# Other queues and another order for the first loads and first products of a graph layer kernel

## Chip, core and metric

One NeuronCore of a Trainium2 chip runs the kernel. The metric is the device time of one execution, in microseconds (us).

## What is computed

64 graphs of 128 nodes, 256 features each, dense weighted adjacency, fp32. Shortened from the reference:

```python
def L0(X, A):                                   # graph attention, 3 hops
    Xw = X @ Wv + bv
    sj, si = Xw @ aw[:d, 0], Xw @ aw[d:, 0]
    e = leaky_relu(sj[:, None, :] + si[:, :, None] + ab[0], 0.2)
    alpha = A * exp(e)
    transition = alpha / (sum(alpha, -1, keepdims=True) + 1e-12)
    H, Xk = 0, X
    for k in range(3):
        H = H + Xk @ Wk[k] + bk[k]
        Xk = einsum('bij,bjd->bid', transition, Xk)
    return relu(H)
x = layernorm(x + L0(x, adj))
x = layernorm(x + einsum('bnm,bmf->bnf', adj, x) @ w)
```

## The kernel before, in words

The 64 graphs are worked on in 32 pairs (`PAIRS`, `PER = 2`). The hops are computed from the inside: H is X W0 + T (X W1 + T (X W2)) with T the transition matrix, so "hop 2" is X times Wk[2], "hop 1" X times Wk[1] added to alpha times that, "hop 0" X times Wk[0] added to alpha times the sum. The projection Wv is folded with the vector aw into two columns u (`ps_u`, `score_weights()`), which stand as columns 256 and 257 of W1 and WY, so that a hop's product gives the scores too; the constant part of the scores is `shift`. The steady products run in pairs of rounded numbers: each fp32 operand is split into a high part (`_hi`, fp32r) and a rest (`_lo`), and three products stand for one (`product()`, L1050). The first pair's hops are made from the unsplit fp32 operands (`first_hop2()`, `first_hop1()`, `first_product()` L1075), which takes two instructions for each product and chunk.

There is no loop at run time. Every engine has its own list of instructions, written out by hand and held together by semaphores:

- SyncE (L304 to L394) issues nearly all loads and stores, in order; a wait ahead of a load holds all loads behind it.
- ScalarE (L397 on) issues four loads at its start (WY_sb, vectors, bk, ab), then makes the high parts (`xt_hi`, `wx_hi`, `v2_hi`, `alpha_hi_of`), the scores, Prelu (`leaky_of`) and Exp (`exponentials`).
- VectorE (L591 on) makes the low parts (`v2_lo`, `v1_lo`, WX_lo, WY_lo), scales by row sums, adds residuals, gathers statistics. Its first instructions, ahead of its helpers, copy `ps_u` and split WY and W0 (L594 to L603).
- GpSimd (L904 on) writes the identity matrix and constants, the ones columns of V2_hi, the products for the shift (L1022 to L1028), then XT_lo (L951), alphas of pairs from 1 on and small normalisation steps.
- TensorE (L1049 on) starts with nine warm-up products of constants (`keep_warm`, L1211), then the first pair as in L1295 to L1313, then `step(k)` for each pair.

The loads of pair 0 and the weights: SyncE loads xt(0), WvT, W1 (`load_Wk(1)`), waits for xt(0), loads W0, xt(1), waits for WY, loads adjs(0), waits for W1, and loads the rest. `y_done` counts hop 2 of a pair, `v1_done` hop 1, `u_done` and `u_ready` the columns u, `bias_done` the sum of the biases (a product of ones and bk). `some` is a constant of ones.

Of the kernel before, what the change touches and what calls it, by code (L numbers as in the profile page):

```python
# [5 lines left out]
F32 = mybir.dt.float32  # L6
F32R = mybir.dt.float32r
ALU = mybir.AluOpType
ACT = mybir.ActivationFunctionType

P = 128
PER = 2
DMA = 16
# [5 lines left out]
def resnorm_graph_kernel(nc, xt, adjs, nodes, WvT, vectors, ab, Wk, bk, w, si_rows, out):  # L19
    PAIRS = nodes.shape[0]  # L20
    D = w.shape[0]
# [4 lines left out]
    with ExitStack() as ctx:  # L26
# [277 lines left out]
        def _(sp):  # L304
            def load_xt(k):
                if k == 4:

                    sp.wait_ge(v1_done, 1)
                if k >= 4:
                    sp.wait_ge(xt_lo_ready, k - 3)  # L310
                sp.dma_start(xt_sb[k % 4][:], xt[k]).then_inc(xt_loaded[k % 4], DMA)
# [38 lines left out]


            load_xt(0)
            sp.dma_start(WvT_sb[:], WvT.rearrange("(c p) n -> p c n", p=P)).then_inc(WvT_loaded, DMA)
            load_Wk(1)
            sp.wait_ge(xt_loaded[0], DMA)
            load_Wk(0)
# [38 lines left out]

        @block.scalar
        def _(act):  # L397
            act.dma_start(WY_sb[:, :, 0:D], Wk[2].rearrange("(c p) n -> p c n", p=P)).then_inc(Wk_loaded[2], DMA)
            act.dma_start(vectors_sb[:].rearrange("p c n -> p (c n)"), vectors).then_inc(vectors_loaded, DMA)
            act.dma_start(bk_sb[:], bk).then_inc(bk_loaded, DMA)  # L400
            act.dma_start(ab_col[:], ab.partition_broadcast(P)).then_inc(ab_loaded, DMA)

            def xt_hi(k):

                act.wait_ge(xt_loaded[k % 4], loads(k, 4))
                act.activation(XT_hi[k % 7][:].rearrange("p c b i -> p (c b i)"),  # L406
                               xt_sb[k % 4][:], ACT.Copy).then_inc(xt_hi_ready, 1)

            def wx_hi(n):
                act.wait_ge(Wk_loaded[n], DMA)  # L410
                act.activation(WX_hi[:, :, 1 - n], (W0_sb, W1_sb)[n][:, :, 0:D], ACT.Copy).then_inc(WX_hi_ready[n], 1)
# [6 lines left out]
            def first_scores():  # L418

                act.wait_ge(v1_done, 1)  # L420
                act.wait_ge(shift_ready, 1)
                act.activation(scores[0][:].rearrange("p n b -> p b n"), ps_v[:, :, D:D + 2], ACT.Identity,
                               bias=shift[:]).then_inc(scores_ready, 1)

            def v2_hi(k):
                if k == 0:
                    act.wait_ge(y_done, 1)

                act.activation(V2_hi[k % 4][:, :, 0:D], hop2(k)[:, :, 0:D], ACT.Copy).then_inc(v2_hi_ready, 1)
# [13 lines left out]
            def exponentials(k):  # L443
                act.wait_ge(leaky_ready, k + 1)
                if k == 1:
                    act.wait_ge(first_alpha_ready, 1)
                if k > 1:
                    act.wait_ge(alpha_ready, k - 1)
                act.activation(exps[:], leaky[:], ACT.Exp).then_inc(exp_ready, 1)  # L449
# [103 lines left out]
                    late_sum_of(LAST - 3)  # L553

            xt_hi(0)
            wx_hi(0)
            v2_hi(0)
            xt_hi(1)
            first_scores()
            xt_hi(2)  # L560
            leaky_of(0)
            exponentials(0)
            xt_hi(3)
            alpha_hi_of(0)
            wx_hi(1)
            scores_of(1)
            v2_hi(1)
# [22 lines left out]
        @block.vector  # L590
        def _(dve):  # L591
            dve.memset(ones[:], 1.0).then_inc(ones_ready, 1)

            dve.wait_ge(u_done, 1)  # L594
            dve.tensor_copy(W1_sb[:, :, D:D + 2], ps_u).then_inc(u_ready, 1)
            dve.tensor_copy(WY_sb[:, :, D:D + 2], ps_u).then_inc(u_ready, 1)
            dve.wait_ge(u_ready, 2)
            dve.wait_ge(Wk_loaded[2], DMA)
            dve.tensor_copy(WY_hi[:], WY_sb[:]).then_inc(WY_hi_ready, 1)
            dve.wait_ge(WY_hi_ready, 1)  # L600
            dve.tensor_tensor(WY_lo[:], WY_sb[:], WY_hi[:].bitcast(F32), ALU.subtract).then_inc(WY_ready, 1)
            dve.wait_ge(WX_hi_ready[0], 1)
            dve.tensor_tensor(WX_lo[:, :, 1], W0_sb[:], WX_hi[:, :, 1].bitcast(F32), ALU.subtract).then_inc(WX_ready[0], 1)  # L603

            def shift_of_scores():
                dve.wait_ge(shift_done, 1)
                dve.wait_ge(ab_loaded, DMA)
# [245 lines left out]
            def split_w():  # L853
# [2 lines left out]
                dve.wait_ge(w_hi_ready, 1)  # L856
                dve.tensor_tensor(w_lo[:], w_sb[:], w_hi[:].bitcast(F32), ALU.subtract).then_inc(w_ready, 1)

            shift_of_scores()
            v2_lo(0)  # L860
            bias_of_hops()
            first_hop1()
            first_alpha()
            first_hop0()
            first_alpha_lo()
            v2_lo(1)
            inverse(0)
            first_v()
# [33 lines left out]

        @block.gpsimd
        def _(pool):  # L904
            pool.memset(identity[:], 0.0).then_inc(pool_setup, 1)
            pool.wait_ge(pool_setup, 1)
            pool.affine_select(out=identity[:], in_=identity[:], compare_op=ALU.not_equal, fill=1.0, base=0,
# [141 lines left out]
        def _(pe):  # L1049
# [242 lines left out]
                    aggregate(k - 1)  # L1292
                hop2_and_scores(k + 5, [1] if k == 1 else range(PER))

            keep_warm(ps_v[:, 0], 9)  # L1295
            first_hop2(0)
            score_weights()
            first_hop2(1)
            first_hop1(0)
            score_shift()  # L1300
            first_hop1(1)
            sum_of_biases()
            pe.wait_ge(identity_ready, 1)
            spread_scores(0)
            hop0(0)
            hop2_and_scores(1)
            pe.wait_ge(ones_columns_ready, 1)
# [59 lines left out]
```

## Time and profile before

| | us |
|---|---|
| median of 3 runs | 275.37 |
| lowest, highest | 274.53, 275.59 |
| profiled execution, its own time | 274.77 |
| its span, first to last instruction | 273.0 |

The profile shows one execution. Times in its rows are us from the start of the span unless marked ns. PE is TensorE (PEld its weight loads), DVE VectorE, ACT ScalarE, POOL GpSimd, SP SyncE; a q behind a name is the engine's queue of issued transfers. A row of a timeline has start, duration, engine, line, operation, output and inputs, count, and in brackets the idle time before it and what ended it. Matmuls are pipelined: a row lasts longer than the step to the next.

| engine | busy us | share of the span |
|---|---|---|
| TensorE | 266.3 | 98% |
| VectorE | 218.0 | 80% |
| ScalarE | 187.8 | 69% |
| GpSimd | 194.8 | 71% |

### The profile page before, as it was taken

Reading aid. Unit: us, or ns where it says so; the run is one execution under the profiler, and the core shown is the slowest. Engines: PE = TensorE matmul, PEld = TensorE weight load, DVE = VectorE, ACT = ScalarE, POOL = GpSimd, SP = SyncE. Lnnn points to the kernel's source line nnn. Section 1 sums busy time; section 2 is a strip of 40 time slices with the busy share of each in tenths; the row PEclk is TensorE's granted clock in tenths of the full one; section 3 lists DMA queues with packets and bytes.
Section 4 is the critical chain, followed back from the end, with each engine's and each line's share of the span. In section 5 each row is a group of like instructions: output and inputs, shape, how many; then the busy total and the mean of one; then the engine's idle time right before and its main releaser. Section 6 shows DMA issues by size and latency. Waiting matters only on the chain.

```text
span 273.0 us, 6038 instructions
## 1 busy us (share of the span) xinstructions
PE 266.3 (98%) x1899; PEld 247.3 (91%) x1899; DVE 218.0 (80%) x613; ACT 187.8 (69%) x427; POOL 194.8 (71%) x419
## 2 busy tenths in 40 slices
PE   7999999999999999999999999999999999999992
PEld 4899999999999999999999999999999999999991
DVE  0877698888889888888988888898888889688984
ACT  2788667777666777766677776667777666666652
POOL 2566548777877777787777878777788877557664
PEclk9999999999999999999999999999999999999999
DMA  7958347647488389454973488654994449722304
GB/s 209 275 174 95 73 115 123 141 117 149 151 144 117 100 135 148 155 154 143 135 97 104 150 154 148 137 156 89 90 168 90 117 115 115 115 66 77 118 2 154
DMA packets 28614, 34.91 MB, mean 128 GB/s; under 512 B 7075, under 2 KB 16422, under 8 KB 28582
## 3 DMA queue, kind: packets, MB, share of 16 engines
q1 hardware_dynamic: 27872, 33.99, 59.3%
q10 hardware_dynamic: 710, 0.53, 0.6%
q8 instruction: 15, 0.25, 0.4%
q14 instruction: 17, 0.14, 0.3%
HBM read 26.09 MB, written 8.42 MB: 126 GB/s over the span
## 4 chain that ended last, share of the span: by engine, by line
PE 94%; DVE 2%; DMA 2%; POOL 0%; issue 0%; ACT 0%; DVEq 0%
PE ps_v L1053 30%; PE ps_y L1053 16%; PE ps_out L1053 14%; PE ps_h L1053 11%; PE ps_agg L1224 10%; PE ps_v L1161 3%; PE ps_v L1165 3%; PE ps_v L1163 3%; DMA WY_sb<-Wk_dram 2%; PE ps_agg L1053 1%; PE ps_y L1079 1%; PE ps_v L1079 1%; DVE WX_lo L870 0%; DVE ps_v L634 0%; PE ps_y L1208 0%; POOL late_rstd L989 0%
## 5 line engine op out<-in xcount | busy, mean ns | idle before, releaser
L963 POOL TENSOR_TENSOR alpha<-exps,adjs 128x256 f32<-128x256 f32 x31 | 22.9, 738 | 35.4 <-ACT exps L449 35.4
L1053 PE MATMUL ps_v<-WX_hi,XT_hi 128*128 128x512 f32 (+1 forms) x128 | 47.7, 372 | 0.0
L1053 PE MATMUL ps_v<-WX_lo,XT_hi 128*128 128x512 f32 (+1 forms) x128 | 47.4, 371 | 0.0
L1053 PE MATMUL ps_v<-WX_hi,XT_lo 128*128 128x512 f32 (+1 forms) x128 | 47.3, 370 | 0.0
L951 POOL TENSOR_TENSOR XT_lo<-xt,XT_hi 128x512 fp32r<-128x512 f32 x32 | 41.5, 1297 | 3.0 <-ACT XT_hi L406 1.6
L481 ACT ACTIVATE y<-res,offset,rstd 128x256 f32<-128x256 f32 x62 | 33.6, 591 | 0.9 <-POOL offset L922 0.9
L967 POOL TENSOR_TENSOR alpha_lo<-alpha,alpha_hi 128x256 fp32r<-128x256 f32 x31 | 22.8, 736 | 15.9 <-ACT alpha_hi L458 15.9
L1053 PE MATMUL ps_y<-WY_hi,XT_hi 128*128 128x258 f32 x112 | 34.1, 304 | 0.0
L1224 PEld LDWEIGHTS ps_agg<-adjs,y 128*128 128x128 f32 x248 | 32.0, 191 | 2.2
L1224 PE MATMUL ps_agg<-adjs,y 128*128 128x128 f32 x248 | 32.6, 274 | 0.0
L1053 PE MATMUL ps_out<-w_hi,agg_hi 128*128 128x256 f32 x112 | 31.6, 282 | 0.0
L1053 PE MATMUL ps_y<-WY_hi,XT_lo 128*128 128x258 f32 x112 | 31.6, 282 | 0.0
L1053 PE MATMUL ps_y<-WY_lo,XT_hi 128*128 128x258 f32 x112 | 31.5, 282 | 0.0
L1053 PE MATMUL ps_out<-w_hi,agg_lo 128*128 128x256 f32 x112 | 31.3, 280 | 0.0
L1053 PE MATMUL ps_out<-w_lo,agg_hi 128*128 128x256 f32 x112 | 31.3, 279 | 0.0
L466 ACT ACTIVATE ps_v<-ps_v,inv_rowsum 128x256 f32<-128x256 f32 x62 | 25.1, 444 | 8.7 <-DVE inv_rowsum L659 6.3
L474 ACT ACTIVATE V_hi<-ps_v 128x512 fp32r<-128x512 f32 x32 | 19.0, 595 | 16.4 <-PE ps_v L1053 16.2
L945 POOL TENSOR_SCALAR out_sb<-res,rstd,offset 128x256 f32<-128x256 f32 x54 | 30.0, 564 | 0.1
L1053 PEld LDWEIGHTS ps_v<-WX_hi,XT_lo 128*128 128x128 f32 x128 | 24.1, 188 | 4.6
L654 DVE TENSOR_SCALAR rowsum<-ps_v 128x2 f32<-128x2 f32 x32 | 5.0, 158 | 28.0 <-PE ps_v L1165 27.9
L1053 PEld LDWEIGHTS ps_v<-WX_hi,XT_hi 128*128 128x128 f32 x128 | 24.1, 188 | 3.6
L1053 PEld LDWEIGHTS ps_v<-WX_lo,XT_hi 128*128 128x128 f32 x128 | 24.1, 188 | 3.4
(168 smaller groups left out, 843.9 us busy)
## 6 DMA issues: line engine op xcount, KB each, us to landing
xt<-xt_dram SPq DMA_DIRECT2D x32, 256.0 KB, 5.9
nodes<-nodes_dram SPq DMA_DIRECT2D x32, 256.0 KB, 6.1
out_dram<-out_sb SPq DMA_DIRECT2D x30, 256.0 KB, 5.9
adjs<-adjs_dram SPq DMA_DIRECT2D x32, 128.0 KB, 6.0
spread<-si_rows_dram SPq DMA_DIRECT2D x29, 128.0 KB, 5.3
W_sb<-Wk_dram SPq DMA_DIRECT2D x2, 256.0 KB, 3.9
si_rows_dram<-scores SPq DMA_DIRECT2D x29, 1.0 KB, 4.1
WY_sb<-Wk_dram ACTq DMA_DIRECT2D x1, 256.0 KB, 4.1
```

Source lines behind the costliest of these rows:

```text
L466: act.activation(ps_v[:, b, 0:D], ps_v[:, b, 0:D], ACT.Copy, scale=inv_rowsum[k % 2][:, b:b + 1]).then_inc(v_scaled, 1)
L474: act.activation(V1_hi[:], ps_v[:, :, 0:D], ACT.Copy).then_inc(v1_hi_ready, 1)
L481: last = act.activation(y[k % 3][:, b], res1[:, b], ACT.Identity, bias=offset1[:, b:b + 1], scale=rstd1[:, b:b + 1])
L945: last = pool.tensor_scalar(out_sb[k % 3][:, b], res2[k % 2][:, b], rstd2[k % 3][:, b:b + 1], offset2[k % 3][:, b:b + 1], ALU.mult, ALU.add)
L951: pool.tensor_tensor(XT_lo[k % 7][:].rearrange("p c b i -> p (c b i)"), xt_sb[k % 4][:], XT_hi[k % 7][:].rearrange("p c b i -> p (c b i)") ...
L963: pool.tensor_tensor(alpha[:], exps[:], adjs_sb[k % 5][:], ALU.mult).then_inc(alpha_ready, 1)
L967: pool.tensor_tensor(alpha_lo[k % 2][:], alpha[:], alpha_hi[k % 2][:].bitcast(F32), ALU.subtract).then_inc(alpha_lo_ready, 1)
L1053: last = pe.matmul(to, a, b, start=start and n == 0, stop=stop and n == 2, skip_group_check=True)
L1161: pe.matmul(ps_v[:, b, 0:D + 2], alpha_hi[k % 2][:, b], V2_hi[k % 4][:, b], start=True, stop=False, skip_group_check=True)
L1163: pe.matmul(ps_v[:, b, 0:D], alpha_hi[k % 2][:, b], V2_lo[k % 4][:, b], start=False, stop=False, skip_group_check=True)
L1165: last = pe.matmul(ps_v[:, b, 0:D + 2], alpha_lo[k % 2][:, b], V2_hi[k % 4][:, b], start=False, stop=False, skip_group_check=True)
L1224: last = pe.matmul(agg(k)[:, c, b], y[k % 3][:, b, c * P:(c + 1) * P], adjs_sb[k % 5][:, b], start=True, stop=True, skip_group_check=True)
```

## The change

The loads of vectors, bk and ab move from ScalarE's queue to GpSimd's, ahead of its constants, in the order bk, vectors, ab. WvT moves from SyncE's queue to ScalarE's, ahead of WY. TensorE's order for pair 0 becomes: seven warm-up products, sum of the biases, scores' weights, shift, one warm-up product, hop 1 of both graphs, hop 2 of graph 0, transposed scores, hop 2 of graph 1. ScalarE and VectorE are reordered to match: the first scores ahead of WX_hi, the sum of biases and the shift ahead of the split of WY, hop 1's copy ahead of the split of W0. SyncE waits for hop 2 of pair 0 ahead of the load of xt(4).

```diff
             def load_xt(k):
                 if k == 4:
 
+                    sp.wait_ge(y_done, 1)
                     sp.wait_ge(v1_done, 1)
...
             load_xt(0)
-            sp.dma_start(WvT_sb[:], WvT.rearrange("(c p) n -> p c n", p=P)).then_inc(WvT_loaded, DMA)
             load_Wk(1)
...
         def _(act):
+            act.dma_start(WvT_sb[:], WvT.rearrange("(c p) n -> p c n", p=P)).then_inc(WvT_loaded, DMA)
             act.dma_start(WY_sb[:, :, 0:D], Wk[2].rearrange("(c p) n -> p c n", p=P)).then_inc(Wk_loaded[2], DMA)
-            act.dma_start(vectors_sb[:].rearrange("p c n -> p (c n)"), vectors).then_inc(vectors_loaded, DMA)
-            act.dma_start(bk_sb[:], bk).then_inc(bk_loaded, DMA)
-            act.dma_start(ab_col[:], ab.partition_broadcast(P)).then_inc(ab_loaded, DMA)
...
             xt_hi(0)
+            first_scores()
             wx_hi(0)
-            v2_hi(0)
             xt_hi(1)
-            first_scores()
-            xt_hi(2)
             leaky_of(0)
             exponentials(0)
+            v2_hi(0)
+            alpha_hi_of(0)
+            xt_hi(2)
             xt_hi(3)
-            alpha_hi_of(0)
             wx_hi(1)
...
             dve.memset(ones[:], 1.0).then_inc(ones_ready, 1)
-
-            dve.wait_ge(u_done, 1)
-            dve.tensor_copy(W1_sb[:, :, D:D + 2], ps_u).then_inc(u_ready, 1)
...
-            dve.tensor_tensor(WX_lo[:, :, 1], W0_sb[:], WX_hi[:, :, 1].bitcast(F32), ALU.subtract).then_inc(WX_ready[0], 1)
-
...
+            dve.wait_ge(u_done, 1)
+            dve.tensor_copy(W1_sb[:, :, D:D + 2], ps_u).then_inc(u_ready, 1)
+            dve.tensor_copy(WY_sb[:, :, D:D + 2], ps_u).then_inc(u_ready, 1)
+            bias_of_hops()
             shift_of_scores()
+            dve.wait_ge(u_ready, 2)
+            dve.wait_ge(Wk_loaded[2], DMA)
+            dve.tensor_copy(WY_hi[:], WY_sb[:]).then_inc(WY_hi_ready, 1)
+            dve.wait_ge(WY_hi_ready, 1)
+            dve.tensor_tensor(WY_lo[:], WY_sb[:], WY_hi[:].bitcast(F32), ALU.subtract).then_inc(WY_ready, 1)
+            first_hop1()
+            dve.wait_ge(WX_hi_ready[0], 1)
+            dve.tensor_tensor(WX_lo[:, :, 1], W0_sb[:], WX_hi[:, :, 1].bitcast(F32), ALU.subtract).then_inc(WX_ready[0], 1)
+            first_alpha()
             v2_lo(0)
-            bias_of_hops()
-            first_hop1()
-            first_alpha()
+            first_alpha_lo()
             first_hop0()
-            first_alpha_lo()
             v2_lo(1)
...
         def _(pool):
+
+            pool.dma_start(bk_sb[:], bk).then_inc(bk_loaded, DMA)
+            pool.dma_start(vectors_sb[:].rearrange("p c n -> p (c n)"), vectors).then_inc(vectors_loaded, DMA)
+            pool.dma_start(ab_col[:], ab.partition_broadcast(P)).then_inc(ab_loaded, DMA)
             pool.memset(identity[:], 0.0).then_inc(pool_setup, 1)
...
-            keep_warm(ps_v[:, 0], 9)
+            keep_warm(ps_v[:, 0], 7)
+            sum_of_biases()
+            score_weights()
+            score_shift()
+            keep_warm(ps_v[:, 0], 1)
+            first_hop1(0)
+            first_hop1(1)
             first_hop2(0)
-            score_weights()
-            first_hop2(1)
-            first_hop1(0)
-            score_shift()
-            first_hop1(1)
-            sum_of_biases()
             pe.wait_ge(identity_ready, 1)
             spread_scores(0)
+            first_hop2(1)
             hop0(0)
```

## Rows read from the trace of the kernel before

**Rows 1.** The page's busy times: us, share of the span, instructions of each engine.

```profile
PE 266.3 (98%) x1899; PEld 247.3 (91%) x1899; DVE 218.0 (80%) x613; ACT 187.8 (69%) x427; POOL 194.8 (71%) x419
```

**Rows 2.** TensorE by stretches: stretch, its us, busy, granted clock, DMA share, GB/s.

```profile
30.00:70.00 40.00, 40.00 (x279) 1.00 0.62 135
```

**Rows 3.** Chain that ended last, in order of time, 0 to 20 us: start, us, what.

```profile
0.73 4.13 DMA WY_sb<-Wk_dram
...
4.99 1.10 PE ps_y L1079 x4
6.10 0.82 PE ps_out L1247 x8
6.91 0.97 PE ps_y L1079 x4
7.88 0.87 PE ps_v L1079 x4
8.76 0.12 PE ps_agg L1254 x2
8.87 0.98 PE ps_v L1079 x4
9.85 0.62 PE ps_agg L1260 x2
10.47 0.36 PE ps_out L1143 x2
10.84 1.43 PE ps_h L1053 x12
12.27 1.45 PE ps_agg L1053 x12
...
18.03 0.98 PE ps_h L1053 x6
```

**Rows 4.** SyncE's queue in the timeline, then issue to landing: transfers by tile.

```profile
1.16 0.42 SPq L353 DMA_DIRECT2D WvT_sb<-WvT_dram  x1
6.46 0.81 SPq L311 DMA_DIRECT2D xt<-xt_dram  x2
...
WvT_sb<-WvT_dram SPq DMA_DIRECT2D x1, 256.0 KB, 4.5
out_dram<-last_out_sb SPq DMA_DIRECT2D x2, 128.0 KB, 2.0
vectors_sb<-vectors_dram ACTq DMA_DIRECT2D x1, 3.0 KB, 4.6
...
DMA to landing us min/median/max: 3.0/3.9/4.8
```

**Rows 5.** Timeline of GpSimd and VectorE, 0 to 10 us.

```profile
0.71 0.20 POOL L905 MEMSET identity<- 128x128 f32 x1 [0.29 <-POOLq L1358]
5.89 0.20 POOL L1023 TENSOR_TENSOR bv_aw<-vectors_sb 128x4 f32<-128x4 f32 x1 [4.06 <-DMA vectors_sb<-vectors_dram]
6.44 0.19 POOL L1028 TENSOR_TENSOR bv_aw_sum<-bv_aw_chunks 128x1 f32<-128x1 f32 x1
6.95 0.16 DVE L595 COPY W_sb<-ps_out 128x4 f32<-128x4 f32 x1 [5.98 <-PE ps_out L1247]
9.11 1.48 POOL L951 TENSOR_TENSOR XT_lo<-xt,XT_hi 128x512 fp32r<-128x512 f32 x1 [1.26 <-ACT XT_hi L406]
```

**Rows 6.** Timeline of the warm-up's end: weight loads and the last product.

```profile
3.27 0.15 PEld L1214 LDWEIGHTS ps_v<-const-bfloat16-1.0 128*128 128x128 bf16 x1 [0.28 <-issue]
3.70 0.12 PEld L1214 LDWEIGHTS ps_v<-const-bfloat16-1.0 128*128 128x128 bf16 x1 [0.28 <-issue]
...
3.94 0.38 PE L1214 MATMUL ps_v<-const-bfloat16-1.0 128*128 128x512 bf16 x1
```

**Rows 7.** Timeline of ScalarE and VectorE: first scores and the two splits of W.

```profile
8.79 0.69 DVE L603 TENSOR_TENSOR WX_lo<-W_sb,WX_hi 128x512 fp32r<-128x512 f32 x1
9.89 0.26 ACT L422 ACTIVATE scores<-ps_v,shift 128x4 f32<-128x4 f32 x1 [0.85 <-PE ps_v L1079]
16.31 1.06 DVE L870 TENSOR_TENSOR WX_lo<-W_sb,WX_hi 128x512 fp32r<-128x512 f32 x1
```

More of the change, by code:

```diff
@@ L592, in _ @@
             dve.memset(ones[:], 1.0).then_inc(ones_ready, 1)
-            dve.wait_ge(u_done, 1)
-            dve.tensor_copy(W1_sb[:, :, D:D + 2], ps_u).then_inc(u_ready, 1)
[L596 to L602, printed above, removed]
-            dve.tensor_tensor(WX_lo[:, :, 1], W0_sb[:], WX_hi[:, :, 1].bitcast(F32), ALU.subtract).then_inc(WX_ready[0], 1)
             def shift_of_scores():
```

## The prediction

> **What bounds the kernel now.** I read the page's busy shares first: TensorE is busy in 98% of the span, VectorE in 80% [rows 1]. Then the busy time by stretches: from 30 to 70 us TensorE is busy in 40.00 of 40.00 us [rows 2], and the four 40 us stretches behind it read the same. So the kernel is TensorE's list of products, and a change of its beginning moves the end only by the idle time or the number of products it takes from or adds to that list. Third, the chain that ended last, in its first 18 us [rows 3]: it starts with the load of WY_sb, 0.73 + 4.13 = 4.86 us, and is TensorE's from 4.99 to 13.71 us without a break: hop 2 of graph 0 (1.10 us), scores' weights (0.82), hop 2 of graph 1 (0.97), hop 1 of graph 0 (0.87), the shift (0.12, between them), hop 1 of graph 1 (0.98), biases (0.62), transposed scores (0.36), hop 0 (1.43), hop 2 and scores of pair 1 (1.45). That is 8.72 us. Behind it the chain leaves TensorE for ScalarE and VectorE and comes back at 18.03 us. That stretch of 4.32 us starts from the end of hop 2 of pair 1 and holds the same instructions in the same order in both kernels.
>
> So one number decides: when hop 2 and scores of pair 1 end, now 13.71 us. All that follows moves with it one to one.
>
> **The products ahead of it.** The change adds and removes no product with data. It takes the biases and the scores' weights ahead of all else, where TensorE now has warm-up products. The warm-up loses two and gets one back. Let T be the start of the first product of hop 1. From T on come all the products of the list but weights, shift and biases: 8.72 - 0.82 - 0.12 - 0.62 = 7.16 us. Hop 2 of pair 1 ends at T + 7.16, and the change breaks even at T = 13.71 - 7.16 = 6.55 us. The 0.62 us of the biases may hold some waiting for the scores behind them, which would put break-even up to about 0.15 us later; I leave that out.
>
> **What T waits for.** Two things, and the later one counts.
>
> The weights W1. They are now the third load of SyncE's queue, landing took 4.8 us, the longer of the two loads into W_sb, and the queue's next loads, which wait for them, start at 6.46 [rows 4]: landed at about 6.43. They become the second, in the place of WvT, which now lands 1.16 + 4.5 = 5.66 us. But in that place WvT had only WY_sb beside it, which was over at 4.86; now ScalarE's queue carries 256 KB of WvT and then 256 KB of WY_sb, and W1 shares the engines with both. The same four loads of 256 KB are in flight, so the last of them should again end near 6.43, and W1 and WY_sb end almost together. Ends: 5.66 and 6.43. I take 6.3, near the upper end.
>
> The scores' weights. They need WvT, vectors and, since the biases stand ahead of them in order, bk. WvT takes over the place of WY_sb as first load of ScalarE's queue, same size and same 1 KB rows: 4.86 us [rows 3]. After the latest of the three comes the 0.82 us of their own. VectorE then copies ps_u, from 6.95 to 7.11, starting 0.04 us after TensorE's part that ends at 6.91 [rows 3, 5], so u is there 0.20 us after its products. GpSimd's three products for the shift took from 5.89 to 6.44 + 0.19 = 6.63, 0.74 us after vectors [rows 5], and are hidden behind the 0.82. The shift (0.12) and one warm-up product (under 0.24, the step from 3.70 to 3.94 us [rows 6]) cover the copy. With V for the latest load and 0.1 us for starting, T is at V + 0.1 + 0.82 + 0.35 = V + 1.27.
>
> V depends on GpSimd's queue, which no row shows: the kernel issues no transfer there. Bounds from the nearest rows: vectors, 3 KB, took 4.6 us behind the 256 KB of WY_sb on one queue and landed about 1 us after it (GpSimd starts on it at 5.89 [rows 5], against 4.86); the shortest transfer of the trace, 128 KB at the quiet end, took 2.0 us [rows 4]. GpSimd's first instruction of the kernel proper starts at 0.71 us [rows 5], and bk goes ahead of vectors. If an issue costs like SyncE's (0.42 us) and the landing 2.0 us, vectors are there at 0.7 + 0.4 + 2.0 = 3.1 us and V is WvT's 4.86. If an issue takes as long as GpSimd's longest ordinary instruction (1.48 us, [rows 5]) and the landing 4.6 us, it is 0.7 + 1.5 + 4.6 = 6.8 us. I take 5.2 us: nearer the quick end, because the two loads come first on an empty queue, before the engines carry much. That gives T = max(6.3, 5.2 + 1.27) = 6.47, so 0.08 us earlier than break-even.
>
> The Trainium skill speaks against any gain from the queue: "DMA: Bandwidth & Descriptors", section "SWDGE vs HWDGE vs iDMA", says that transfers from all issuing engines end up on the same 16 engines, and its "Specifications" put the first byte of a GpSimd transfer at about 1 us, against 0.6 us for SyncE and ScalarE. An estimate by these figures alone puts vectors a few tenths of a us later than on another queue, which alone would leave V between 4.9 and 5.5. No row here shows it.
>
> **What is moved elsewhere.** Each has a cover. ScalarE loses three issues and gets one, ahead of a first activation that needs xt; the biases' products and the weights' use no result of it. GpSimd's setup moves behind three issues; identity is wanted after T + 3.6, the columns of ones after T + 7. The small biases' copy and the shift on VectorE fall in time that it idled. On SyncE's queue the wait for WY_sb ahead of adjs(0) ends about 1.6 us later (6.43 for 4.86); adjs(0) is wanted by the first alpha, behind the first scores, their transposes, Prelu and Exp, so not before T + 3.9 = 10.4 us. Loads of the start took 3.0 to 4.8 us [rows 4], so it lands between 9.5 and 11.3: alpha may wait up to 0.9 us, and its user on TensorE, propagate_v2(0), comes at T + 7.2, which covers it; without that cover it would cost those 0.9 us. Loading xt(4) now waits for hop 2 of pair 0 too, which ends at T + 4.0 where hop 1 ends at T + 2.0; adjs(3), nodes(1) and the later xt stand behind it on the queue. All of them are for pairs 1 and 3 to 7, and the earliest, xt(4), is read only behind alpha_hi(1), after hop 2 of pair 1.
>
> The tightest new wait is WX_lo for hop 0. ScalarE makes WX_hi(0) only after the first scores (0.26 us), VectorE subtracts after first_hop1, a pass over 128x512 like the one of 0.69 us at 8.79 [rows 7]. Worked from T: hop 1 ends at T + 2.0, scores at T + 2.3, first_hop1 ends at T + 3.0, WX_lo at T + 3.7 if it takes 0.69 us too, at T + 4.05 if it takes 1.06 us as at 16.31 [rows 7]. Hop 0 may start at T + 1.95 + 1.95 = T + 3.9 or so (four products with the transposes between). So between 0 and 0.2 us are lost; I take 0, by the nearer row, 8.79, in which GpSimd was at XT_lo just as it will be here. XT_lo of pair 1 follows WX_hi on ScalarE and takes GpSimd 1.48 us: about T + 4.9, wanted at T + 5.7.
>
> Scores, exponentials and alpha_lo of pair 0 come earlier against TensorE's list. The pause that this takes away (about 0.1 us ahead of the first product with alpha) isn't worth anything: the chain there runs over V_lo and not over alpha.
>
> **Sum.** 6.47 - 6.55 = -0.08 us; the 0.15 us left out above makes it -0.1 to -0.2. Profiled execution: 274.77 us, of that 273.0 span and 1.77 around it. 274.77 - 0.15 = 274.62. The median of the runs is 0.60 above the profiled one, so I predict 275.37 - 0.15 = 275.2 us.
>
> **Rivals.**
> 1. GpSimd's loads are late (slower). At the long bound, 6.8 us, T = 8.07, and the time is 8.07 - 6.55 = +1.5 us, 276.9. It is slower by over 0.5% (1.38 us) from V = 6.66 us. For it: the quickest load into W_sb took 3.0 us, and the small one of vectors 4.6. Against: nothing is queued ahead of GpSimd's loads. In full 0.12; its milder part (V of 5.6 to 6.6, +0.3 to +1.3 us) another 0.12.
> 2. TensorE's clock. All stretches read a granted clock of 1.00 [rows 2], yet the warm-up products, 512 columns each, start 0.43 us apart (3.27, 3.70), which is 1.2 GHz, and the last follows after 0.24 us, 2.4 GHz [rows 6]. The step came at about 3.7 us, after 2.9 us of uninterrupted products, and seven of them end at just that moment. If bk isn't there then and the clock stays low into hop 1, its two calls cost 0.87 + 0.98 us more: 277.0. Against: in the kernel before, the pause from the last warm-up product (ended at 4.32 us) to 4.99 did not bring the clock down: four instructions of hop 2 took 1.10 us there and 0.97 at 6.91 [rows 3, 6]. 0.10. The Trainium skill's "TensorE: Matmul & The Clock Gate", Part 1, says that the low rate is the default and activity releases it, which is what these rows show.
> 3. All at its best (faster): W1 at 5.66, V at 4.86, T = 6.13, -0.4 us, and if the pause before 18.03 closes too, -0.6 us: 274.7. Nothing brings 1.38 us, for WvT alone holds T at 6.13. 0.10.
> 4. The forecast itself, a change that does nothing or close to it: T between 6.3 and 7.0, -0.25 to +0.45 us. 0.56.
>
> **How the numbers follow.** A measurement of this kernel tells about 0.5% from no change, 1.38 us. Same: cases 3 and 4, the milder part of 1 and a little of 2: 0.77. Slower: 0.12 and most of 0.10, so 0.20. Faster by more than that: 0.03, for what the bounds overlook. The range: the three runs of before spread over 1.06 us, so the low end is 275.37 - 0.6 and 0.4 below, 274.4. The high end takes in rival 1 up to its bound of 276.9; beyond it lie about 0.13.
>
> **What would show it.** In the timeline after: the biases before 5 us; the first product of hop 1 at 6.3 to 7.0 us; hop 2 of pair 1 ending T + 7.2, near 13.6 us, and the chain back on TensorE 4.3 us later. Wrong would be: vectors landing after 5.6 us, f32 products of 128x258 stepping at double length after 5 us, a pause ahead of hop 0 over 0.3 us (WX_lo, adjs), or any change between 30 us and the end.

## The result, and the profile after

The changed kernel takes 279.09 us (median of 5; 277.53 to 279.37) where the kernel before takes 274.82 (median of 5). The medians lie 4.3 us apart. The ratio, 1.0137 with a 95% interval of 1.0119 to 1.0155, goes by the means, which lie 3.8 us apart: slower by 1.4%. Several kernels below have executions of two kinds, some at 274 to 276 us and some at 277 to 279, and the sections on them count both, for the difference is the subject; one execution each of b_pool and a_fill2 was disturbed throughout and is left out, the second with its trace. The profiled execution of the changed kernel is the quickest of its five, 277.53 us with a span of 275.7; a second trace, of an execution at 279.41, follows as an experiment.

The page, busy us of each engine, then the granted clock in 40 slices:

```profile
PE 267.7 (97%) x1898; PEld 248.5 (90%) x1898; DVE 217.6 (79%) x613; ACT 187.7 (68%) x427; POOL 196.5 (71%) x422
PEclk9799999999999999999999999999999999999998
```

Against [rows 1] TensorE has 1.4 us more of busy time and GpSimd 1.7; nothing else stands out. The second slice of the clock, 6.9 to 13.8 us, reads 7. By stretches of 2 us (stretch, its us, busy, granted clock, DMA share, GB/s), and one of the steady part, all engines:

```profile
6.00:8.00 2.00, 2.00 (x12) 0.82 0.83 262
8.00:10.00 2.00, 2.00 (x6) 0.50 0.92 319
10.00:12.00 2.00, 2.00 (x9) 0.83 0.93 321
...
30.00:70.00 40.00, 40.00 (x282) 37.26 (x281) 32.10 (x92) 28.61 (x67) 28.45 (x59) 1.00 0.60 124
```

The steady part is full as in [rows 2]. Nearly everything is lost in the first 20 us. The chain there (start, us, what), which answers to [rows 3]:

```profile
1.26 4.54 DMA bk_sb<-bk_dram
...
5.94 0.66 PE ps_agg L1261 x2
6.60 1.15 PE ps_out L1248 x8
7.76 0.43 PE ps_agg L1255 x2
8.18 0.45 PE ps_v L1215
8.63 2.83 PE ps_v L1080 x8
...
16.07 0.52 ACT WX_hi L409
...
20.56 0.98 PE ps_h L1054 x6
```

The chain comes back to TensorE at 20.56 us where it came at 18.03: 2.53 us later, of 2.76 us between the two profiled executions. It begins with bk and no longer with WY_sb; hop 1's eight instructions take 2.83 us where they took 0.87 + 0.98. It also leaves TensorE earlier, at the end of hop 1 (8.63 + 2.83 = 11.46 us), and runs over ScalarE until WX_hi at 16.07, where the chain of [rows 3] stays on TensorE up to the end of hop 2 of pair 1. GpSimd's issues and TensorE's wait, from the timeline, and issue to landing (the last number), against [rows 4] and [rows 5]:

```profile
1.26 0.74 POOL L903 DMA_DIRECT2D bk_sb<-bk_dram  x1 [0.82 <-POOLq L1360]
2.00 0.59 POOL L904 DMA_DIRECT2D vectors_sb<-vectors_dram  x1
...
5.94 0.66 PE L1261 MATMUL ps_agg<-bk_sb,ones 3*128 3x256 f32 x2 [2.03 <-DMA bk_sb<-bk_dram]
6.07 0.20 POOL L1024 TENSOR_TENSOR bv_aw<-vectors_sb 128x4 f32<-128x4 f32 x1 [1.81 <-DMA vectors_sb<-vectors_dram]
...
bk_sb<-bk_dram POOLq DMA_DIRECT2D x1, 3.0 KB, 4.5
vectors_sb<-vectors_dram POOLq DMA_DIRECT2D x1, 3.0 KB, 4.0
```

Seven warm-up products end at 3.9 us, bk lands at 5.80, vectors at 6.0: TensorE pauses for 2.03 us and then starts with data 0.95 us later than before, and not with hop 2, whose products have 256 output columns, but with the biases and the scores' weights. The weights and the shift are narrow products, of two columns and one; the text below calls them so, and those of the hops and the warm-up wide.

### The profile page after: what moved, and what is told of

The parts are those of the page before. It is cut to its first block, busy times and chain, and to the rows that moved or that the text cites. A ratio compares the mean times of both kernels' runs of the same rounds, so it can differ in the third digit from the quotient of the medians.

```text
span 275.7 us, 6036 instructions
## 1 busy us (share of the span) xinstructions
PE 267.7 (97%) x1898; PEld 248.5 (90%) x1898; DVE 217.6 (79%) x613; ACT 187.7 (68%) x427; POOL 196.5 (71%) x422
## 4 chain that ended last, share of the span: by engine, by line
PE 92%; DVE 2%; ACT 2%; DMA 2%; issue 1%; POOL 0%; DVEq 0%; POOLq 0%
PE ps_v L1054 29%; PE ps_y L1054 16%; PE ps_out L1054 14%; PE ps_h L1054 11%; PE ps_agg L1225 10%; PE ps_v L1162 3%; PE ps_v L1166 3%; PE ps_v L1164 3%; DMA bk_sb<-bk_dram 2%; PE ps_v L1080 1%; PE ps_agg L1054 1%; ACT XT_hi L404 0%; PE ps_out L1248 0%; ACT WX_hi L409 0%; DVE ps_v L620 0%
```

## The experiments

Two questions: how much of the 4.3 us is the late start and how much the clock, and what makes each. Times stand beside executions of the kernel before in the same batch, medians of 274.79 to 274.94 us; of all those executions none is above 275.64.

### The changed kernel again

> The changed kernel unaltered. Its five times were 277.53 once and 278.8 to 279.4 four times, and the only trace is of the 277.53. Theory A (the loads of GpSimd are late, and TensorE's clock falls in the pause that this makes): a trace of an execution near 279 shows the same first product at 5.9 us, and a longer stretch in which f32 products step at double length than the 7.3 to 10.7 us of the trace at hand, worth the missing 1.5 us. Theory B (the loads alone, the clock plays no part): the first product with data comes 1.5 us later, near 7.5 us, and the steps are the same.

279.24 us (278.83 to 279.41), ratio 1.0158 (1.0141 to 1.0175). The chain of an execution at 279.41, and one stretch of TensorE:

```profile
6.18 1.19 PE ps_agg L1261 x2
7.37 1.80 PE ps_out L1248 x8
9.17 0.42 PE ps_agg L1255 x2
9.60 0.45 PE ps_v L1215
10.04 3.31 PE ps_v L1080 x8
...
22.43 0.98 PE ps_h L1054 x6
...
8.00:10.00 2.00, 2.00 (x10) 1.00 0.84 298
```

Everything from the first product runs at half speed: the biases 1.19 for 0.66 us, the weights 1.80 for 1.15 and, in the kernel before, 0.82, hop 1 3.31 for 1.85. The full clock comes at about 12.9 us only. The granted clock reads 1.00 all the while; it is the durations that tell the 1.2 GHz, as the warm-up's steps of 0.43 us did in [rows 6]. So theory A's longer stretch at half speed is there, and B falls. But theory A let the clock fall in the pause, and neither trace shows that. In the one of 279.41 it had not risen at all: the seven warm-up products step at 0.43 us like those of [rows 6] up to 3.70. In the trace of the 277.53 the seven are as slow, the first product behind the pause is at full speed at 5.94 us, and the clock fell at about 7.3, in the weights, and rose at 10.7.

### More warm-up products

```diff
-            keep_warm(ps_v[:, 0], 7)
+            keep_warm(ps_v[:, 0], 17)
```

> The changed kernel with 17 warm-up products in place of 7, so that TensorE is busy until bk lands near 5.8 us (7 at 0.43 us end at 3.8, 10 more at 0.22 us end near 6.0). Theory A: no product with data runs at the low clock, the scores' weights take 0.82 us again and hop 1's eight instructions 1.85 instead of 2.83 us, hop 1 starts near 7.6; the time falls to 276.0 to 276.6, what stays over 274.8 is the lateness of the loads. Theory B: the time stays at 278.5 to 279.5, since the loads land no earlier.

> The changed kernel with 13 warm-up products. 17 ended at 6.87 us, 0.9 us behind bk's landing near 5.9. With 13 they end near 5.9 where the clock rises early, later where it rises late. Theory A: 275.7 to 276.3, 0.5 to 0.8 below the run with 17, if the clock still holds; if the clock needs the longer warm-up, single executions of 278 to 279 appear.

With 17: 276.54 us (276.04 to 276.99), ratio 1.0061 (1.0041 to 1.0082). With 13: 276.15 us, five executions of 275.92 to 276.53 and one of 277.78; ratio 1.0055 (1.0033 to 1.0077). The chain with 13:

```profile
0.77 5.35 PE ps_v L1215 x13
...
6.15 0.67 PE ps_agg L1261 x2
6.81 0.98 PE ps_out L1248 x8
...
8.26 1.88 PE ps_v L1080 x8
...
19.23 0.98 PE ps_h L1054 x6
```

Hop 1 is back at 1.88 us, and 3 of the 4.3 us are gone without any load being earlier. What is left, 19.23 - 18.03 = 1.20 us in the chain and 276.15 - 274.80 = 1.35 us in the medians, is the late start. So the loss is 1.3 us of late start and 3 us of clock. The late start has two parts that this run doesn't separate, the landing of the loads and the new order. With 17 products the last ended at 6.87 us, after bk, and that costs 0.4 us more.

### Fewer warm-up products in the kernel before

```diff
-            keep_warm(ps_v[:, 0], 9)
+            keep_warm(ps_v[:, 0], 7)
```

> The kernel before with 7 warm-up products in place of 9, nothing else. The pause ahead of the first product with data grows from 0.67 to about 1.2 us. Theory A in its weak form (it takes the 2.0 us pause of the changed kernel to lose the clock): 274.8, as before. If already two fewer products cost the clock: 276 to 278, with products at double step behind 5 us.

> The kernel before with 5 warm-up products. With 7, single executions were 274.6 to 274.8 or 277.8 to 279.0, and the profiled one was of the first kind. With 5 the second kind should be caught in a trace: f32 products of hop 2 and hop 1 at double step behind 5 us, the scores' weights at 1.7 us or more, 277.5 to 279.5. Theory B (no role of the clock): 274.8, since the first product with data waits for WY until 4.9 us in either case.

With 7: of ten executions four took 274.56 to 274.79 us and six 277.84 to 278.98; median 277.99. With 5: 278.41 and 278.43, ratio 1.0129 (1.0102 to 1.0156). My weak form of theory A is wrong: it does not take a pause of 2 us. Two warm-up products less cost the clock in six of ten executions; the pause was 0.95 us in the trace, which is of one of the other four. The chain with 5:

```profile
4.69 2.04 PE ps_y L1079 x4
6.73 1.50 PE ps_out L1247 x8
8.23 1.91 PE ps_y L1079 x4
10.15 1.72 PE ps_v L1079 x4
```

These are the products of [rows 3] at double duration, 1.91 for 0.97 and 1.72 for 0.87, though the first of them starts earlier than before (4.69 for 4.99). With 5 the edit costs 3.5 us and with 7 the medians differ by 3.2, of the change's 4.3, without touching a load or an order.

### The queue alone

The kernel before with the three small loads on GpSimd's queue:

```diff
-            act.dma_start(vectors_sb[:].rearrange("p c n -> p (c n)"), vectors).then_inc(vectors_loaded, DMA)
-            act.dma_start(bk_sb[:], bk).then_inc(bk_loaded, DMA)
-            act.dma_start(ab_col[:], ab.partition_broadcast(P)).then_inc(ab_loaded, DMA)
...
+            pool.dma_start(bk_sb[:], bk).then_inc(bk_loaded, DMA)
+            pool.dma_start(vectors_sb[:].rearrange("p c n -> p (c n)"), vectors).then_inc(vectors_loaded, DMA)
+            pool.dma_start(ab_col[:], ab.partition_broadcast(P)).then_inc(ab_loaded, DMA)
```

> The kernel before with only the three small loads moved to GpSimd's queue, all orders as before. bk and vectors should land near 5.8 and 6.0 us as in the changed kernel, against 5.83 for vectors before. Theory A: within 0.3 us of before, 274.6 to 275.2; the queue by itself is no loss, it only does not bring the loads early, and the loss comes from making TensorE's first product wait for them. Rival C (a third queue costs by itself, at the start or at the end of the kernel): 276 or more.

275.53 us (nine executions), ratio 1.0033 (1.0012 to 1.0053), with two executions at 277.06 and 277.33. That is between the 275.2 that theory A allowed at most and the 276 of rival C. Even in the old order the queue is a small loss: vectors land at 6.33 us, not earlier than 5.83, and TensorE waits 0.40 us for them:

```profile
6.37 1.05 PE L1247 MATMUL ps_out<-vectors_sb,WvT_sb 128*128 128x2 f32 x8 [0.40 <-DMA vectors_sb<-vectors_dram]
```

### Why the small loads are late

```diff
+            sp.wait_ge(ab_loaded, DMA)
             load_xt(0)
...
+            act.wait_ge(ab_loaded, DMA)
             act.dma_start(WvT_sb[:], WvT.rearrange("(c p) n -> p c n", p=P)).then_inc(WvT_loaded, DMA)
```

> The changed kernel with the first loads of SyncE and ScalarE held back until ab has landed, so that GpSimd's three loads run on empty engines. Only their landing is read; the time is several us longer. Theory D (the 4.0 to 4.8 us from issue to landing are the other queues' traffic): bk and vectors land in 2.0 to 2.5 us. Theory E (they are a price of this queue): 3.8 us or more as with traffic. Half and half would be near 3.2.

One execution, 281.57 us; only the landings are read. With nothing else in flight (issue to landing last):

```profile
bk_sb<-bk_dram POOLq DMA_DIRECT2D x1, 3.0 KB, 2.0
vectors_sb<-vectors_dram POOLq DMA_DIRECT2D x1, 3.0 KB, 1.9
```

2.0 and 1.9 us against 4.5 and 4.0 with the others' traffic: theory D. The queue itself adds 0.55 us ahead of its first issue (1.26 for [rows 5]'s 0.71) and 0.74 and 0.59 us for the issues. The Trainium skill, "DMA: Bandwidth & Descriptors", section "SWDGE vs HWDGE vs iDMA", says that transfers of all issuing engines interleave on the same 16 DMA engines; these two rows agree with it. Here the biases, which need bk alone, ended at about 5.1 us, the weights waited for WvT until 8.92, and all products to 15 us ran at half speed.

### The small loads first on ScalarE's queue

```diff
+            act.dma_start(bk_sb[:], bk).then_inc(bk_loaded, DMA)
+            act.dma_start(vectors_sb[:].rearrange("p c n -> p (c n)"), vectors).then_inc(vectors_loaded, DMA)
             act.dma_start(WvT_sb[:], WvT.rearrange("(c p) n -> p c n", p=P)).then_inc(WvT_loaded, DMA)
             act.dma_start(WY_sb[:, :, 0:D], Wk[2].rearrange("(c p) n -> p c n", p=P)).then_inc(Wk_loaded[2], DMA)
+            act.dma_start(ab_col[:], ab.partition_broadcast(P)).then_inc(ab_loaded, DMA)
...
-            pool.dma_start(bk_sb[:], bk).then_inc(bk_loaded, DMA)
-            pool.dma_start(vectors_sb[:].rearrange("p c n -> p (c n)"), vectors).then_inc(vectors_loaded, DMA)
-            pool.dma_start(ab_col[:], ab.partition_broadcast(P)).then_inc(ab_loaded, DMA)
```

> The changed kernel with the small loads at the head of ScalarE's queue (bk, vectors, then WvT, WY, ab) and none on GpSimd's; all orders of the engines as changed. If lateness comes from GpSimd's queue (issue starts at 1.27 us and costs 0.74 and 0.59), bk lands by 4.0 us and vectors by 4.5, WvT by 5.5; the biases' product starts near 4.1, hop 1 near 7.0; and 7 warm-up products are enough in most executions: 275.0 to 276.0. If it comes from the traffic, both land at 5 us or later, the pause of 2 us and the low clock stay, and the time is 278.5 or more.

> Small loads at the head of ScalarE's queue, as in the run at 278.1, with 10 warm-up products in place of 7. bk (under 3.8 us) and vectors (4.4) are there early, WvT at 5.3. 10 products end at 4.7 us or later, then the biases, so that nothing pauses for more than 0.2 us ahead of the weights. Theory A: in executions where the clock rises in the warm-up, hop 1 starts at 6.6 to 6.9 us and the time is 274.5 to 275.1, level with before; if it does not rise (as with 7, where it stayed low to 11.4 us though the pause was 0.37 us), 277 to 278.5.

With 7 warm-up products: 278.10 us (277.29 to 278.74). With 10 (the edit of `keep_warm` alone): 275.71, six executions of 274.79 to 275.89, three of 277.25 to 277.46 and one of 279.42; in its trace, of 277.25, WvT landed only at 6.16 us and the pause was 0.94. bk was there without a pause and WvT, at 5.28 us, made one of 0.37 us in the trace with 7; yet hop 1 took 3.44 us. So with 7 the start was earlier and the clock was still low. The pause, which my prediction and theory A held responsible, isn't the whole cause.

### The orders with the queues of before

> The orders of the changed kernel on all engines and 13 warm-up products, but the queues of the kernel before (WvT second on SyncE's, W1 third; WY, vectors, bk, ab on ScalarE's, none on GpSimd's). vectors landed at 5.8 us there, bk behind it, W1 at 6.4. Theory G (the loss that is left with a full clock comes from the order, which puts hop 2's product with data, possible from 5.0 us, behind loads of 5.8 us and more, and not from GpSimd's queue): 275.7 to 276.5, like the changed queues with 13 warm-up products (276.15). If GpSimd's queue made it: 275.0 or less.

276.35 us, four executions of 275.61 to 276.42 and 277.20 and 277.48; ratio 1.006 (1.0039 to 1.0081). The four have a median of 276.15, the same as the full-clock executions with the changed queues and 13 products: theory G. The order costs also without GpSimd's queue, for it puts hop 2's products, possible from 5.0 us, behind loads of 5.5 us and more. That the queue costs nothing is not shown: here the biases start at 5.62 us and in the trace with the changed queues at 6.15, four and five executions that spread over 0.8 and 0.6 us can't settle that half microsecond, and b_pool's median lay 0.7 us above the kernel before. The profiled execution is of the second kind. TensorE's timeline and, by 1 us stretches, its clock:

```profile
0.76 4.57 PE L1215 MATMUL ps_v<-const-bfloat16-1.0 128*128 128x512 bf16 x13 [0.76 <-PEq L1360]
5.62 0.67 PE L1261 MATMUL ps_agg<-bk_sb,ones 3*128 3x256 f32 x2 [0.29 <-DMA bk_sb<-bk_dram]
6.22 1.05 PE L1248 MATMUL ps_out<-vectors_sb,WvT_sb 128*128 128x2 f32 x8
...
7.70 3.48 PE L1080 MATMUL ps_v<-W_sb,xt 128*128 128x258 f32 x8
...
7.00:8.00 1.00, 1.00 (x7) 0.71 0.96 213
8.00:9.00 1.00, 1.00 (x3) 0.50 0.92 287
```

The clock was full at 5.6 us, the only pause was 0.29 us, and it fell at about 7.4, behind 1.1 us of narrow products. These alone are not the cause either: in the trace with the changed queues the same ones follow 13 warm-up products at a full clock, and it held.

There are thus two ways to lose the clock, and the record tells them apart. In the three traces in which it fell and rose again (277.53, this one and the one of 277.25 with 10 products) the mean granted clock of the execution is 0.990 or 0.991. In those in which it stayed low from the start (279.41 above, 277.86 of the small loads on ScalarE's queue with 7, 278.43 with 5) it is 0.997 or 0.998, since the low start reads as full. All executions of the kernel before have 0.995 or more. By this mark the six long ones of b_warm7 (0.997 to 0.999) were low from the start, and b_pool's 277.06 and 277.33 (0.991 both) and the 277.78 with 13 products (0.991) were falls. Of the changed kernel's nine, six were low from the start and three show a fall (277.53, 279.09 and 279.15, with 0.990, 0.986 and 0.987). Against the executions of the same kernel at a full clock, a fall costs 1.2 to 2.0 us (here, b_pool, 13 products, 10 products) and a low start 3.5 to 3.9 (b_warm7, and a_best2 below).

The traces also differ in when the clock rose. Where it fell in the narrow products, it had risen by 4.1 us (here, where 13 warm-up products take 4.57 us and not 5.35, and with 10) or in the pause before 5.9. Where it held through them, in the traces of a_warm17 and a_warm13, it rose at 5.4 us. That goes with the fall in these few traces; why is not shown.

### ScalarE's order

With 13 warm-up products, and in ScalarE's list:

```diff
             xt_hi(2)
-            xt_hi(3)
-            wx_hi(1)
             scores_of(1)
             v2_hi(1)
+            xt_hi(3)
+            wx_hi(1)
```

> As the run with 13, and ScalarE makes the scores and V_hi of pair 1 ahead of XT_hi of pair 3 and WX_hi of hop 1, which held it until 16.0 us (17 warm-ups) while TensorE's product was there at about 15.75. Theory F (the changed order makes ScalarE the link behind hop 2 of pair 1): 0.1 to 0.25 us less than the run with 13. If WX_hi is then late for V_lo's chain instead: the same or up to 0.5 us more.

277.61 us; two executions at 276.77 and 276.82, at a full clock, two at 278.39 and 278.49. The better pair is 0.6 us above the 276.15 of the run with 13. This order wins nothing. The chain shows where it goes:

```profile
16.30 0.63 ACT WX_hi L409
16.93 0.52 ACT leaky L437 x2
...
17.97 1.03 POOL alpha L964
...
20.26 1.26 POOL XT_lo L952
...
21.56 1.70 PE ps_y L1054 x12
```

The scores of pair 1 are made at 15.14, but WX_hi then stands ahead of `leaky_of(1)`, and alpha, alpha_lo and XT_lo of pair 4 follow late. XT_hi of pair 3 is later too, and TensorE idles 0.40 us ahead of 17.89 for its XT_lo. There was next to nothing to win. In the run with 13, hop 2 of pair 1 ended at 15.08 us, and ScalarE began the scores behind it at 15.17:

```profile
15.17 0.24 ACT L413 ACTIVATE scores<-ps_agg,shift 128x4 f32<-128x4 f32 x1
```

That is 0.09 us, against 0.03 us in the kernel before (13.74 behind 13.71). Theory F falls: ScalarE stands on the chain and holds it up by 0.06 us. The other two executions, at 278.39 and 278.49, show a granted clock of 0.991 and 0.990, so theirs fell.

### The changed order with early loads

vectors at the head of SyncE's queue, WvT, bk, WY, ab on ScalarE's, and the weights ahead of the biases:

```diff
+            sp.dma_start(vectors_sb[:].rearrange("p c n -> p (c n)"), vectors).then_inc(vectors_loaded, DMA)
             load_xt(0)
...
-            keep_warm(ps_v[:, 0], 7)
-            sum_of_biases()
+            keep_warm(ps_v[:, 0], 9)
             score_weights()
+            sum_of_biases()
             score_shift()
```

> The changed order with each load where it lands early: vectors first on SyncE's queue, WvT first on ScalarE's, bk behind it; 9 warm-up products, the weights ahead of the biases. vectors near 3.9 us, WvT near 4.4, weights from 4.5, biases, shift, one warm-up product, hop 1 when W1 is there, near 6.4 to 6.7 us, where break-even is about 6.87. 274.3 to 274.9 with a full clock: 0 to 0.5 us faster than before. If the weights, 128x2 products, do not keep the clock: 276 or more.

Twelve executions: seven of 274.19 to 274.61 us, one of 276.02, four of 278.05 to 278.46. The seven are 0.3 to 0.75 us below the kernel before (274.94 in this batch); the mean of all is 0.9 above it. Landings, then the warm-up and hop 1 in the trace (one of the four):

```profile
WvT_sb<-WvT_dram ACTq DMA_DIRECT2D x1, 256.0 KB, 3.0
vectors_sb<-vectors_dram SPq DMA_DIRECT2D x1, 3.0 KB, 1.7
...
0.76 4.00 PE L1215 MATMUL ps_v<-const-bfloat16-1.0 128*128 128x512 bf16 x9 [0.76 <-PEq L1360]
...
8.15 3.65 PE L1080 MATMUL ps_v<-W_sb,xt 128*128 128x258 f32 x8
```

TensorE never paused, and the clock didn't fall: it had not risen when the narrow products began. The nine warm-up products take 4.00 us, all at 0.43 us steps, where they take 3.56 in the trace of before, and hop 1 is at half speed throughout. Nine warm-up products as in the kernel before, no pause, and still the low clock in five of twelve (by the mean granted clock four were low from the start and one, at 276.02 us with 0.992, fell).

Three kernels then add warm-up products to this one. The first two add four, behind each product of the weights or in one block ahead (`keep_warm` 13); the third adds two, each behind a chunk's first product:

```diff
                     for j in range(C):
                         last = pe.matmul(ps_u[:, c], WvT_sb[:, j, c * P:(c + 1) * P], vectors_sb[:, j, 0:2],
                                          start=j == 0, stop=j == C - 1, skip_group_check=True)
+                        if True:
+                            keep_warm(ps_v[:, 0], 1)
```

> As a_best2 (9 warm-up products, weights first, quick loads, no pause), with one warm-up product of 512 columns behind each of the four products of 128x2 that make the scores' weights. Theory H (the clock is not raised, or lost, in the stretch of narrow products, though TensorE never pauses): no execution near 278, all at 274.4 to 275.2 (0.86 us more work than a_best2, part of which waits for W1 anyway). Theory A (only pauses cost the clock, a_best2 had none, so its executions at 278 have another cause): a third of the executions stays at 278.

> As a_best2 with 13 warm-up products in one block in place of 9: the same number of extra products as a_fill4. Theory H: executions of 277 to 278.5 remain, fewer than in a_best2 (4 of 12 at 278, one at 276), since the narrow products still stand in one block behind the warm-up. Theory I (the sum of the warm-up decides, not where it stands): none remain, as in a_fill4. Quick executions: 274.4 to 275.2.

> As a_fill4 with two fillers, behind the first product of each chunk. Theory H: few or no executions near 278; the quick ones at 274.2 to 274.7, level with a_best2's quick ones, because the 0.43 us of fillers fit ahead of W1. If it holds it is 0.1 to 0.2% faster than before.

Four between: 274.54 to 276.07, median 275.59. Four ahead: 274.85 to 276.30, median 275.52; both ratios 1.0022 (1.0011 to 1.0034), and none of 2 x 12 executions near 278. Two between: nine of 274.41 to 275.18, two at 278.70 and 278.87. By these counts theory I: four extra products took the low clock from five of twelve to none wherever they stand. Two in eleven against five in twelve is too few to tell what two of them do. The four cost what the early loads had brought.

### One early load without the changed order

```diff
+            sp.dma_start(vectors_sb[:].rearrange("p c n -> p (c n)"), vectors).then_inc(vectors_loaded, DMA)
             load_xt(0)
...
-            act.dma_start(vectors_sb[:].rearrange("p c n -> p (c n)"), vectors).then_inc(vectors_loaded, DMA)
```

> The kernel before with one edit: vectors (3 KB) goes from ScalarE's queue to the head of SyncE's, ahead of xt(0). In a_best2 the first load of ScalarE's queue landed 3.0 us after its issue with that neighbour, against 4.1 in before, and xt(0) near 4.4 us. So WY and xt(0) should both be there at about 4.4 us, hop 2 starts near 4.6 instead of 4.99, all else as before. Theory H (wide products with data directly behind the warm-up hold the clock): no execution above 276, 274.4 to 274.7, up to 0.4 us below before. If the queues or the length of the pause decided: some executions near 278.

275.22 us (274.78 to 275.47, eleven executions, none near 278), ratio 1.0012 (1.0003 to 1.0021). Hop 2 did start at 4.54 us, but the weights now wait for WvT (its load from the chain first):

```profile
1.63 4.05 DMA WvT_sb<-WvT_dram
...
4.54 1.13 PE L1079 MATMUL ps_y<-WY_sb,xt 128*128 128x256 f32 x4
...
5.81 1.02 PE L1247 MATMUL ps_out<-vectors_sb,WvT_sb 128*128 128x2 f32 x8
```

WvT lands at 5.68 us, the weights start 0.12 us earlier than before (5.81 for 5.93 in the timeline) and hop 2 of pair 1 ends at 13.64 where it did at 13.71: of the 0.45 us, 0.07 are left. No version beats the kernel before reliably.

Nine warm-up products and then 128x256 products with data: no low clock in any execution of the kernel before or of this one. Nine and then the narrow ones: five of twelve. That comparison supports what theory H said of a_best2, and it changes the order of the products and not the number of the warm-up products; but theory H's own test, the place of the fillers, did not tell it from theory I. The counts of executions with a low clock, all of them:

| warm-up products, then | executions with a low clock |
|---|---|
| 9, wide (before, b_vec) | 0 of all |
| 9, wide, a pause of 0.40 us in the trace, narrow (b_pool) | 2 of 9 |
| 7, wide (b_warm7) | 6 of 10 |
| 5, wide (b_warm5) | 2 of 2 |
| 7, biases and narrow, late loads (the changed kernel) | 9 of 9 |
| 7, biases and narrow, small loads first (a_actfirst) | 4 of 4 |
| 10, the same (a_actfirst10) | 4 of 10 |
| 13, biases and narrow, late loads (a_warm13, a_warm13_act, b_order13) | 5 of 16 |
| 17, the same (a_warm17) | 0 of 4 |
| 9, narrow, early loads (a_best2) | 5 of 12 |
| 9 + 2, narrow, early loads (a_fill2) | 2 of 11 |
| 9 + 4 or 13, narrow, early loads (a_fill4, a_front13) | 0 of 24 |

So 13 products do not make the clock safe in the new order with late loads, and nine wide ones with wide ones behind did not in b_pool. What in the mix decides stays open. That the first microseconds of each execution differ at all, with the same program, is seen (step to full speed at 3.7 us in [rows 6], 5.4 us with 17 products) and not explained.

## Why the prediction was wrong, step by step

The forecast was 275.2 us, between 274.4 and 276.9; measured were 279.09. Two steps failed: V, the landing of the latest small load, 1.3 us of the loss, and the clock, for which the sum has no term at all, 3 us.

**What bounds it, and that only the start counts.** Right. TensorE's steady part is unchanged, and the loss arises before the chain's return to it, 2.5 of 2.76 us between the two profiled executions. The stretch behind hop 2 of pair 1 was to take 4.32 us in both; with 13 warm-up products it took 19.23 - 15.08 = 4.15. The chain ran over ScalarE there from hop 1 on, which I did not foresee and which cost 0.06 us.

**Break-even and T.** The products from T on were put at 7.16 us. With 13 warm-up products T was 8.14 in the timeline and hop 2 of pair 1 ended at 15.08, so 6.94, 0.22 less: a small error, and on the cautious side. With it the late start adds up: 8.14 - 6.55 = 1.59 us behind break-even, less 0.22 of products and 0.17 of the stretch behind them, is the 1.20 us of the chain. The forecast T of 6.47 was wrong by 1.7 us even at a full clock.

**V, the latest load.** This step failed first. I took 5.2 us for V between 4.86 and 6.8, "because the two loads come first on an empty queue, before the engines carry much". The queue was empty and the engines were not: 4.5 and 4.0 us to landing, 2.0 and 1.9 when they were really alone. Bare sizes: first issue at 1.26 us (taken 0.7), issues of 0.74 and 0.59 (taken about 0.4), landing 4.0 (2.0 to 4.6 bounded). With the row of vectors in [rows 4], 4.6 us beside the same traffic, I had the right price and chose the one of the quiet end. Second, V as the latest of three loads left out that the biases' product stands between bk and the weights: bk at 5.80 + 0.14 + 0.66 = 6.60, which is later than vectors at 6.0. So V was in effect 6.5 us in the profile after; with 13 warm-up products, 6.7.

**The rivals.** The loss that happened is rivals 1 and 2 together, which I priced apart and left out of the sum. Rival 1 came nearly to its bound, 1.35 us by the medians. Rival 2 was the larger part, 3 us, where I gave 1.85: I charged two calls of hop 1, but in a typical execution the biases, the weights, the shift and all of hop 1 ran low, from 6.2 to 12.9 us. The sum put the clock at nothing, and rival 2's chance, 0.10, was the gravest error. Its mechanism, a clock that stays low into hop 1, is what happened. The argument against it was that a pause of 0.67 us hadn't brought the clock down in the kernel before. That tells whether a risen clock falls, not whether it rises, and the row has nine warm-up products and wide ones behind; I carried it over to seven and narrow ones. The sentence that "seven of them end at just that moment" was the warning, and I read it as a hazard only if bk was late. b_warm7 shows that it was one in any case: six of ten executions.

**Other waits.** WX_lo was no issue: hop 0 started at 13.29, right behind hop 2 of graph 1. The queues' covers for adjs and xt held. W1 landed by 6.04 us, where the queue's next loads start (6.3 predicted), and did not decide.

**The Trainium skill.** The rule that I quoted against a gain, all queues on the same 16 engines, agrees with what was measured, a landing of 4.5 us beside the others' traffic against 2.0 us without it. Its first-byte figures alone, a few tenths of a us more, would have left V at 4.9 to 5.5 us and missed the effect.

## What to carry to other kernels

A small load is not early because its queue is empty: price its landing by a row taken beside the same traffic, here twice the quiet value. The early landings came where it was issued no later than the large ones: at 0.72 us on SyncE's queue 3 KB took 1.6 to 2.4 us, at 1.26 us on GpSimd's 4.5. When the first products are reordered or the warm-up is cut, judge the clock by the durations of known products, not by the granted clock, and look at several executions: one trace can be of the good kind (b_warm7's was, at 274.79 us, with a median of 277.99). Taking two warm-up products away cost more than everything that the reordering could have won.

## What the runs showed of the hardware that I had not expected

- The granted clock reads 1.00 in stretches where products demonstrably run at half speed, from the start until the clock's first rise: 3.31 us for hop 1 beside 1.00 in the changed kernel. It reads 0.50 only where the clock had been full before and fell (8 to 10 us in the profile after).
- The first full-speed product comes at different times in executions with the same start, 3.7 and 5.4 us here. In the trace of 277.53 the seven warm-up products all step at 0.43 us, nothing runs for 2.03 us, and the next product is at full speed (0.66 us for the biases, 1.19 in the one of 279.41).
- The mean granted clock of an execution tells a fall (0.986 to 0.992) from an undisturbed one (0.995 and more), but not a low start, which reads 0.996 to 0.999.
- GpSimd's first issue started 0.55 us later than its first ordinary instruction did, and its issues took 0.74, 0.59 and 0.55 us, more than the 0.38 to 0.42 of SyncE's first two.
- The same 3 KB load, vectors, took 1.6 to 2.4 us at the head of SyncE's queue, 3.1 and 3.2 us second on ScalarE's, 4.0 to 4.3 us on GpSimd's and 4.3 to 4.6 us behind 256 KB on ScalarE's.
